# Softmax attention on TensorE: value products, projections and new values issued in halves between the products of a pair's two heads

## The reference

```python
x = x + jnp.tanh(g_xattn[0]) * _L0_xattn_ref(_layernorm(x, axis=-1), ctx_2048, ...)   # softmax attention
x = x + jnp.tanh(g_ffn[0]) * _L0_ffn_ref(_layernorm(x, axis=-1), ...)                 # 8 experts, 2 per row
x = x + jnp.tanh(g_xattn[1]) * _L1_xattn_ref(_layernorm(x, axis=-1), ctx_2048, ...)   # linear attention
x = x + jnp.tanh(g_ffn[1]) * _L1_ffn_ref(_layernorm(x, axis=-1), ...)                 # causal attention, 16 experts
```

```python
q = split_heads(_proj(x, Wq, bq)); k = split_heads(_proj(c, Wk, bk)); v = split_heads(_proj(c, Wv, bv))
q = _apply_rotary(q_emb, q); k = _apply_rotary(k_emb, k)
scores = jnp.einsum('bhtc,bhsc->bhts', q, k) / math.sqrt(K_CH)
p_attn = jax.nn.softmax(scores, axis=-1)
out = jnp.einsum('bhts,bhsc->bhtc', p_attn, v)
return _proj(out, Wo, bo)
```

## Time and profile before

| what | value |
|---|---|
| median of 3 executions | 2686.56 us (2667.90 to 2697.57) |
| the profiled execution | 2682.36 us |
| its span, first to last instruction | 2680.6 us |
| TensorE busy over the span | 2266.7 us, 85% |
| granted clock over the span | 0.900 |
| busy time of VectorE, ScalarE, GpSimd | 1855.2, 1159.6, 1103.8 us |

### The profile page before, as it was taken

How to read it: one execution, slowest core, us unless ns; L and a number is a source line. 1 busy time by engine, 2 the same in 40 slices (tenths; PEclk the granted TensorE clock), 3 DMA queues, 4 the chain that set the end, 5 groups by cost and what they waited for, 6 DMA issues and landing times. The chain is left out here.

```text
span 2680.6 us, 60407 instructions
## 1 busy us (share of the span) xinstructions
PE 2266.7 (85%) x20880; PEld 1718.4 (64%) x20880; DVE 1855.2 (69%) x3965; ACT 1159.6 (43%) x2509; POOL 1103.8 (41%) x1111
## 2 busy tenths in 40 slices
PE   6899999885887689995799998999988698999990
PEld 4555555543766567773577877777767577887770
DVE  4888888872556757765778788788787365445754
ACT  2676667664533223333344444444333263333330
POOL 3454445464153500000454454455477600224626
PEclk9897779865888889997999999999989799999995
DMA  5455555442368431201322323322334472446754
GB/s 118 120 115 129 143 129 135 114 125 87 113 215 252 150 134 41 60 29 40 88 66 75 84 66 78 81 72 73 76 96 116 136 240 79 138 137 184 234 159 144
DMA packets 249859, 313.10 MB, mean 117 GB/s; under 512 B 45152, under 2 KB 202848, under 8 KB 249056
## 3 DMA queue, kind: packets, MB, share of 16 engines
q1 hardware_dynamic: 188592, 219.11, 29.3%
q0 software_dynamic: 26624, 58.79, 8.0%
q10 hardware_dynamic: 34352, 31.34, 3.5%
HBM read 122.40 MB, written 102.24 MB: 84 GB/s over the span
## 5 line engine op out<-in xcount | busy, mean ns | idle before, releaser
L2084 POOL TENSOR_TENSOR ca_qk<-ca_qk,ca_q_swap 128x512 f32<-128x512 f32 x160 | 249.3, 1558 | 366.5 <-DVE ca_q_swap L2262 366.2
L731 DVE TENSOR_REDUCE soft_top<-soft_pa 128x2 fp32r<-128x512 f32 x512 | 328.1, 683 | 101.2 <-PE soft_pa L811 98.1
L626 ACT ACTIVATE soft_prob<-soft_pb 128x512 f32<-128x512 f32 x512 | 285.7, 594 | 190.4 <-PE soft_pb L804 187.9
L804 PE MATMUL soft_pb<-soft_rep 25*128 25x256 f32 x1024 | 210.2, 378 | 46.5 <-DVE soft_top L731 27.0
L804 PEld LDWEIGHTS soft_pb<-soft_rep 25*128 25x128 f32 x1024 | 137.3, 225 | 169.6 <-issue 85.3
L1416 PE MATMUL moe_pgu<-moe_w_hi,moe_xt_hi 128*128 x472 | 196.1, 415 | 38.9 <-DVE moe_xt_lo L1333 30.1
L811 PE MATMUL soft_pa<-soft_rep 24*128 24x256 f32 x1024 | 219.2, 384 | 5.8 <-DVE soft_top L731 3.5
L1435 PE MATMUL moe_py<-moe_w_d,moe_at 128*128 x788 | 217.8, 392 | 1.5 <-issue 0.8
L1338 DVE TENSOR_TENSOR moe_act_f<-moe_silu,moe_pgu 128x256 f32<-128x256 f32 (+1 forms) x236 | 88.4, 375 | 151.0 <-ACT moe_silu L1253 150.4
L2353 PE MATMUL ca_py<-ca_w_hi,ca_ot_hi 128*128 128x256 f32 x512 | 157.6, 308 | 35.0 <-DVE ca_ot_lo L2283 34.8
L1253 ACT ACTIVATE moe_silu<-moe_pgu 128x256 f32<-128x256 f32 (+1 forms) x236 | 82.1, 348 | 230.6 <-PE moe_pgu L1416 230.3
(11 more groups left out here) (377 smaller groups left out, 6376.3 us busy)
## 6 DMA issues: line engine op xcount, KB each, us to landing
ca_q_swap<-ca_q_f SPq DMA_DIRECT2D x640, 64.0 KB
moe_xs<-moe_rows SPq DMA_DIRECT2D x236, 128.0 KB, 2.1
soft_rep<-soft_parts SPq DMA_DIRECT2D x378, 64.0 KB
moe_rows<-soft_blank SPq DMA_DIRECT2D x27, 768.0 KB, 3.7
moe_ys_rows<-moe_ys ACTq DMA_DIRECT2D x134, 128.0 KB, 1.7
moe_ys<-moe_ys ACTq DMA_DIRECT2D x102, 128.0 KB, 2.3
moe_xd<-scratch SPq DMA_DIRECT2D x64, 128.0 KB, 2.6
ca_vs<-ca_v SPq DMA_DIRECT2D x32, 256.0 KB, 3.7
```

Of the source, the lines that this page charges most:

```text
L626: act.activation(prob[:, k % 4, h, :], p_b[:, 2 * T * h:2 * T * (h + 1)], ACT.Exp).then_inc(prob_ready, 1)
L731: dve.tensor_reduce(heads[:, j, :, g], p_a[:, 2 * T * h:2 * T * (h + 1)].rearrange("p (c s) -> p c s", c=HALF), AX, ALU.max).then_inc(a_do ...
L804: mm = pe.matmul(p_b[:, out], rep[of, i % 4, g, at:at + PART], rep[of, i % 4, g, 0:T], start=True, stop=True)
L2084: pool.tensor_tensor(qk[:, u % 2, m, :], qk[:, u % 2, m, :], q_swap[:, p % 2, :], ALU.add).then_inc(qk_ready, 1)
```

## The change

Nothing is added or left out: the same products are issued with the same operands. `both` gets the head as an argument, `values` the half `sc`, and `project` the half (queries or keys); the rest is put into functions, and the loop is written out anew. Where before the two heads of a pair stood side by side, in six of the eight pairs (0, 1, 2, 3, 4, 6) something of 128 rows now stands between them; in pairs 5 and 7 the heads are still side by side. The semaphores' counts stay; `values` waits ahead of its first half and tells of its end after the second.

```diff
-                def both(i, k):
+                def both(i, k, h):
...
-                    for h in range(2):
-                        if live(i):
-                            past(pe, prob_ready, 2 * (PAIRS * i + k) + h - 1)
...
-                def values(i, g):
+                def values(i, g, sc):
...
-                    for sc in range(HALF):
-                        for j in range(4):
...
+                    for j in range(4):
...
+                    if sc == HALF - 1:
+                        mm.then_inc(pv_done, 1)
...
-                def project(n, rotated):
+                def project(n, rotated, half):
...
-                for i in every:
-                    both(i, 0)
-                    project(i + 4, False)
-                    both(i, 1)
-                    values(i - 1, 3)
-                    if routed(i - 6):
-                        route.grade(pe, i - 6, 1, p_x[0][:, T:T + 8], turned)
...
+                for i in every:
+                    both(i, 0, 0)
+                    values(i - 1, 2, 1)
+                    both(i, 0, 1)
+                    project(i + 4, False, 0)
+                    both(i, 1, 0)
+                    project(i + 4, False, 1)
+                    both(i, 1, 1)
+                    values(i - 1, 3, 0)
+                    both(i, 2, 0)
+                    values(i - 1, 3, 1)
+                    if routed(i - 6):
+                        route.grade(pe, i - 6, 1, p_x[0][:, T:T + 8], turned)
+                    both(i, 2, 1)
+                    project(i + 4, True, 0)
+                    both(i, 3, 0)
+                    project(i + 4, True, 1)
+                    both(i, 3, 1)
+                    values(i, 0, 0)
+                    both(i, 4, 0)
+                    values(i, 0, 1)
+                    both(i, 4, 1)
+                    new_values(i)
+                    both(i, 5, 0)
+                    both(i, 5, 1)
+                    values(i, 1, 0)
+                    both(i, 6, 0)
+                    values(i, 1, 1)
+                    both(i, 6, 1)
+                    project_out(i)
+                    both(i, 7, 0)
+                    both(i, 7, 1)
+                    routing(i)
+                    values(i, 2, 0)
```

More of the change, by code:

```diff
@@ L784, in _ @@
                 pe.wait_ge(shift_ready, 1)
-                def both(i, k):
+                def both(i, k, h):
                     n, m = (i + 1, k + 4) if k < 4 else (i + 2, k - 4)
-                    if live(i) and k == 0:
+                    if live(i) and k == h == 0:
                         pe.wait_ge(peak_in[i % 2], 64 * (i // 2 + 1))
-                    if live(n) and m == 0:
+                    if live(n) and m == h == 0:
                         pe.wait_ge(rep_in[n % 4], REP * (n // 4 + 1))
-                    for h in range(2):
-                        if live(i):
-                            past(pe, prob_ready, 2 * (PAIRS * i + k) + h - 1)
-                        if live(n):
-                            past(pe, a_done, 2 * (PAIRS * n + m) + h - 1)
-                        for c in range(HALF):
-                            out = slice((2 * h + c) * T, (2 * h + c + 1) * T)
-                            if live(i):
[L802 to L814, removed]
@@ L816, in values @@
-                def values(i, g):
+                    if live(i):
+                        past(pe, prob_ready, 2 * (PAIRS * i + k) + h - 1)
+                    if live(n):
+                        past(pe, a_done, 2 * (PAIRS * n + m) + h - 1)
+                    for c in range(HALF):
+                        out = slice((2 * h + c) * T, (2 * h + c + 1) * T)
+                        if live(i):
+                            g, rows = pair(k)
+                            of, at = slice(32 * rows[h], 32 * rows[h] + SPLIT + 1), T + c * PART
+                            mm = pe.matmul(p_b[:, out], rep[of, i % 4, g, at:at + PART], rep[of, i % 4, g, 0:T],
+                                           start=True, stop=True)
+                            if c == HALF - 1:
+                                mm.then_inc(b_ready, 1)
+                        if live(n):
+                            g, rows = pair(m ^ 1)
+                            of, at = slice(32 * rows[h], 32 * rows[h] + SPLIT), c * PART
+                            mm = pe.matmul(p_a[:, out], rep[of, n % 4, g, at:at + PART], rep[of, n % 4, g, T:2 * T],
+                                           start=True, stop=True)
+                            if c == HALF - 1:
+                                mm.then_inc(a_ready, 1)
@@ L828, in values @@
-                    mm.then_inc(pv_done, 1)
-                def project(n, rotated):
+                    if sc == 0:
+                        pe.wait_ge(prob_ready, 2 * (PAIRS * i + 2 * g + 2))
+                        pe.wait_ge(vaug_ready, i + 1)
+                        past(pe, o_out, GROUPS * i + g - 1)
+                    for j in range(4):
+                        mm = pe.matmul(p_o[g % 2][32 * j:32 * j + 32, 0:T], vaug[:, i % 4, sc, 4 * g + j, :],
+                                       prob[:, (2 * g + j // 2) % 4, j % 2, sc * T:(sc + 1) * T],
+                                       start=(sc == 0), stop=(sc == HALF - 1), tile_position=(0, 32 * j))
@@ L833, in project @@
                     r = int(rotated)
+                    if half == 1:
+                        pe.matmul(p_x[1][:, T:2 * T], w_in[:, 2 + r, :], ct[:, n % RING, :], start=True, stop=True
+                                  ).then_inc(qkrot_ready if rotated else qk_ready, 1)
+                        return
                     if rotated:
@@ L841, in project, with new_values @@
                     pe.matmul(p_x[1][:, 0:T], w_in[:, r, :], xn[:, n % 2, :], start=True, stop=True)
-                    pe.matmul(p_x[1][:, T:2 * T], w_in[:, 2 + r, :], ct[:, n % RING, :], start=True, stop=True
-                              ).then_inc(qkrot_ready if rotated else qk_ready, 1)
-                for i in every:
-                    both(i, 0)
-                    project(i + 4, False)
-                    both(i, 1)
-                    values(i - 1, 3)
-                    if routed(i - 6):
-                        route.grade(pe, i - 6, 1, p_x[0][:, T:T + 8], turned)
[L853 to L858, removed]
+                def new_values(i):
                     n, v = i + 1, i + 3
@@ L867, in _ @@
                         pe.wait_ge(route.map_out, 1)
-                    mm = None
                     if live(n):
@@ L873, in _, with project_out @@
                                            start=True, stop=True)
[L874 to L878, removed]
+                    if live(n) or live(v):
+                        if live(v):
+                            for sc in range(HALF):
+                                mm = pe.matmul(p_x[0][:, sc * PART:(sc + 1) * PART],
+                                               ct[:, v % RING, sc * PART:(sc + 1) * PART], w_in[:, 4, :], start=True, stop=True)
                         mm.then_inc(v_ready, 1)
-                    both(i, 5)
-                    values(i, 1)
-                    both(i, 6)
+                def project_out(i):
                     t = i - 2
@@ L889, in _, with routing @@
                         pe.matmul(p_x[1][:, 0:T], w_out[:], on[:, t % 2, :], start=True, stop=True).then_inc(wo_ready, 1)
-                    both(i, 7)
+                def routing(i):
                     if routed(i - 5) or i in (RANK, RANK + 1):
@@ L899, in _ @@
                         route.map_blocks(pe, p_x[0], ident_f)
-                    values(i, 2)
+                for i in every:
[32 more added lines that the diff above has]
+                    values(i, 2, 0)
 def _rows():
```

6 lines of the change are left out of this document (removed).

## The result

The changed kernel takes 2934.24 us in the median against 2685.80: a ratio of 1.0937 [1.0872, 1.1003], 9.4% slower, some 248 us. The profiled execution took 2932.05 us. The forecast was 2865 us with 2740 to 2905; the direction and the kind of loss were right, the size was 69 us too small, outside the range. The new values, which the title names among what is halved, stand whole in both orders; only the projections and the value products are cut.

What follows compares the result with a forecast made beforehand. TensorE alone was taken to bound tiles at 1.2 GHz, the deciding regime. Tiles +197.5 us, two faster tiles -17 and tail +3 gave +183 on 2682.4, so 2865 us; range 2740 to 2905.

Steps and rivals of the forecast that it cites:

- Two regimes, and the lower one decides: Stage tiles: 17.08 us at 2.4 GHz with waits to fill, 21.45 at 1.2 GHz where TensorE alone sets the time.
- Pairs pulled apart: Six of eight pairs per tile at 1.2 GHz: 1.44 us each instead of 0.73, so 4.3 us more a tile.
- A half costs half.: Projections and values cut in two: each half was taken to cost half the whole piece, adding zero.
- 12 new boundaries: Switches between kinds of array work, 18 to 30 a tile: at most 0.4 us a tile seen, taken as zero.
- the forecast's 744.4 us: The thirty tiles in the split order, all at 1.2 GHz: 620.8 plus 116.1 plus 7.5 us, against 546.90 before.
- The clock does not come back: Once fallen to 1.2 GHz, the clock was expected to stay there for the rest of the stage.
- the two tiles at 2.4 GHz that I had granted (-17 us): Two tiles before the first lasting clock fall, each about 8.5 us cheaper: -17 us.
- my third rival: Faster: waits inside pairs filled, clock never down for long, tiles about 16.2 us, 2620 us in all; chance 0.06.
- The page's slices, which I had reading 5: Granted-clock slices were to read 5 from the second or third slice to the stage's end, meaning 1.2 GHz.
- Start and tail: The stage's tail of 28.42 us, already at 1.2 GHz: half-size pairs wait for ScalarE, +3 us.
- 12 us for the boundaries: Allowance for boundaries between kinds of array work, 30 x 0.4 us, kept only for the range's upper end.
- 620.8 us by the forecast's sum: Thirty tiles in the old order, all at 1.2 GHz: 343.2 plus 218.9 plus 58.7 us.

Runs made afterwards that it cites:

- e4: The changed kernel with six extra whole-array products per tile whose results nobody reads: 2792.2 us, 1.042 of the kernel before.
- e1: The kernel before with six pieces cut in halves as in the change, but no pair pulled apart: 2790.4 us, ratio 1.040.
- e3: The kernel before with only the four values cut and four pairs pulled apart, projections whole: 2786.3 us, ratio 1.043.
- e8: The kernel before, order unchanged, with the same six extra products per tile as e4: 2733.0 us, ratio 1.018.

## Why the prediction came out as it did

- **Two regimes, and the lower one decides.** Right. The forecast rested on TensorE's 21.45 of 21.45 us in the tile at 1.2 GHz; the changed tile is full as well, and the gaps inside pairs at 2.4 GHz had no part in the result.
- **Pairs pulled apart.** Right in size: 0.72 us for four products alone, six pairs, 4.3 us a tile.
- **"A half costs half."** Wrong, and this is the term that failed. The sum put the price of the 12 new boundaries between kinds of work at zero, with 0.03 us each, 0.4 us a tile, as the most that the rows showed. A half projection takes 1.15 and a half `values` 1.01 us, which makes 1.2 us more per tile, 0.1 us for each boundary, or 32 us for 27 tiles. I had read the price from two products that stand inside one piece; what the end of a piece costs is seen only when it is cut. What the thirty tiles have beyond the forecast's 744.4 us and the 17 us of the rank tiles below is 36 us, so the cuts account for nearly all of it. The Trainium skill's rule (TensorEngine Tiling (Array Packing), Key Properties), which I weighed and left out of the sum for want of a figure, points the right way; that the array drains is not shown by these rows, only the price of a cut.
- **The clock does not come back.** Right, and stronger than forecast: it never rose in the stage, so the two tiles at 2.4 GHz that I had granted (-17 us) did not exist. e4 shows by a change of its own that the clock is a cause: more work, a higher grant, a shorter time. Against my third rival, and against the Trainium skill's rule that activity releases the throttle (TensorE: Matmul & The Clock Gate, The HAM clock gate) as it stands, is the row of 797 us with TensorE 98.5% busy at 1.2 GHz. What I had wrong is what it takes: e1 shows that cutting alone is enough for hundreds of microseconds, e3 that four pairs apart are not enough to lose it for good. The page's slices, which I had reading 5, read 9 because the record has no entry there.
- **The rank tiles.** Left out. Three tiles around the ranking take 32.9, 29.2 and 28.6 us, 14 us more than three of 25.6, and three of the routed tiles 28.1, 1 us more each than the others; the sum for the thirty tiles did not hold these 17 us. Two of them in the profile after:

```profile
665.10:698.01 32.91, 32.91 (x180) 19.78 (x178) 14.85 (x25) 12.88 (x28) 8.84 (x13) 1.00 0.27 61
309.76:337.87 28.11, 27.21 (x153) 13.71 (x151) 17.58 (x44) 13.23 (x29) 9.45 (x14) 1.00 0.35 81
```

- **Start and tail.** 4 us more ahead of the first tile, nothing in the tail, where I had 3.

So the term that failed is the cut of the pieces (36 us), with the missing start at 2.4 GHz (17) and the rank tiles (17) behind it. 183 + 36 + 17 + 17, with 4 more at the start, 3 less in the tail and 4.5 less in the later stages, make 249.5 against 249.7 measured; the 36 is a remainder, so that the sum closes is no proof of it, and the rows give 32 by themselves. The upper edge of the range had 12 us for the boundaries; with 36 it would be 2929, and 2934 is reached only with the rank tiles.

Two parts of the loss can be told apart by the tiles. In the old order at 1.2 GHz throughout, the thirty tiles would take 620.8 us by the forecast's sum and 638 with the 17 us that it left out and that stand in both orders. That is 91 us more than the 546.90 they took, and it is the clock. The other 159 are array work that the split adds at that clock, of which at 2.4 GHz only 1.2 us a tile, 36 us, would be left. With the clock up throughout the change would cost some 1.3%. These figures are estimates: the first from the forecast's sum and tiles of the changed kernel, the last from e4 and e8; neither was measured by itself.

## What to carry to other kernels

Products on part of the array's rows are cheap only where products on the other rows stand beside them; something put between to fill a wait of 0.2 us can double their time. Read the kernel's tile at both clock levels before filling gaps: an order that costs about 1.2 us a tile at 2.4 GHz cost 5.7 on 21.5 at 1.2 and kept the clock there. Where the clock keeps falling in a stage with a few thin places in every tile, products over the whole array that nobody reads can pay for themselves at these places: here one at each of two places gained 1.0%, two at one place nothing, and six lost 1.8%.

## What the runs showed of the hardware that I had not expected

- TensorE was busy for 98.5% of 797 us and stayed at 1.2 GHz, in an order in which every projection and every `values` was cut and narrow products stood between the halves; adding 192 products over the whole array to it made the kernel 142 us faster (e4).
- The row of the granted clock shows 1.00 ahead of the first change on record, though the products take the time of 1.2 GHz: 797 us in the changed kernel, 257 us of the thirty tiles in e1, and the first 69 us of the kernel before. The duration of a product of known size (0.58 or 0.38 us here) tells the level where the record doesn't.
- Cutting a piece in two costs 0.29 and 0.15 us at 1.2 GHz: halves of 1.15 and 1.01 us out of pieces of 2.01 and 1.87.
